# Node tiles worked off inside the first edge loop of a two-layer graph network on one Trainium2 core

## What is computed

```python
# layer 0: edge weights from edge_attr_8, messages from f[src], summed at dst
h = gelu(ea8 @ Wfc1 / sqrt(8)); h = gelu(h @ Wfc2 / 8); w = h @ Wfc3 / 8   # w0, w1: 64, w2, w3: 32 columns
gs, gv = f_s[src], f_v[src]; y0, y1 = ea4[:, 0], ea4[:, 1:4]
mid0 = w0 * gs * y0
mid1 = w3 * einsum('euc,ec->eu', gv, y1) / sqrt(3)        # the dot product
mid2 = (w1 * gs)[:, :, None] * y1[:, None, :]
mid3 = w2[:, :, None] * gv * y0[:, None, None]
ns0, ns1, nv2, nv3 = segment_sum(mid*, dst)
res = self_connection(x) + alpha * (sums @ Wl2);  x = layernorm(x + res)
# layer 1: weights from edge_attr_64, messages from x[dst], summed at src
w = relu(ea64 @ W_fc1) @ W_fc2; xs, xv = (x @ W_nl)[dst]; sh = sqrt(3) * ea3 / |ea3|
out = [w0*xs, w3*dot(xv, sh), (w1*xs) sh, w2 xv, w4*cross(xv, sh)]
x = layernorm(x + gate(segment_sum(out, src) / 32 @ W_out + x @ W_skip))
```

## Time and profile before

| | us |
|---|---|
| median of 3 runs | 2751.35 |
| lowest and highest | 2736.01, 2775.7 |
| the profiled execution | 2767.32 |
| its span, first to last instruction | 2765.5 |
| POOL busy | 2063.6 |
| DVE busy | 1649.6 |
| ACT busy | 899.5 |

### The profile page before, as it was taken

The page is one execution under the profiler, slowest core; times in us unless marked ns, Lnnn a source line. Parts: engine busy times, 40 slices in busy tenths (PEclk is TensorE's granted clock), DMA queues, the critical chain, the costliest instruction groups (busy, mean ns, idle before and its releaser), DMA issues.

```text
span 2765.5 us, 80992 instructions
## 1 busy us (share of the span) xinstructions
PE 2655.6 (96%) x24330; PEld 2250.7 (81%) x24330; DVE 1649.6 (60%) x4264; ACT 899.5 (33%) x2015; POOL 2063.6 (75%) x1856
## 2 busy tenths in 40 slices
PE   4799999999999999999999999999999999999996
PEld 2477777777777777979999999999999999999993
DVE  5365555556555555526666666666666666666664
ACT  1111111111111112224444444444444444444442
POOL 3477777777777775247888888888888888888884
PEclk9999799889989898659999999999999999999998
DMA  4343343333433333247888888888888888888877
GB/s 132 111 110 105 100 109 106 100 104 105 108 103 105 105 105 85 104 173 142 141 144 144 141 144 143 144 143 143 143 142 143 143 144 142 144 144 142 144 124 189
DMA packets 388993, 355.59 MB, mean 129 GB/s; under 512 B 60992, under 2 KB 340928, under 8 KB 388416
## 3 DMA queue, kind: packets, MB, share of 16 engines
q0 software_dynamic: 150528, 141.40, 34.9%
q1 hardware_dynamic: 234816, 209.69, 27.2%
q10 hardware_dynamic: 3616, 4.11, 0.6%
HBM read 244.75 MB, written 135.90 MB: 138 GB/s over the span
## 4 chain that ended last, share of the span: by engine, by line
PE 65%; POOL 16%; issue 11%; DMA 3%; DVE 1%; DVEq 0%; ACT 0%; SPq 0%; POOLq 0%; ACTq 0%
POOL gat L693 15%; PE ps_o L1062 13%; PE ps_w L1050 12%; PE ps_d L1071 10%; PE ps_o L1060 9%; PE ps_x L1084 6%; PE ps_g L909 4%; PE ps_x L1024 3%; DMA gat<-f,gidx 2%; PE ps_w L935 2%; PE ps_h L928 1%; PE ps_h L923 1%; PE ps_r L981 1%; DMA tab<-summed,sidx 1%; PE ps_y L998 1%
## 5 line engine op out<-in xcount | busy, mean ns | idle before, releaser
L740 POOL DMA_INDIRECT tab<-summed,sidx x784 | 1218.6, 1554 | 264.5 <-issue 212.7
L693 POOL DMA_INDIRECT gat<-f,gidx x784 | 751.8, 959 | 244.8 <-issue 232.0
L1291 DVE TENSOR_TENSOR prod<-ps_w,xg 128x768 f32<-128x768 f32 x392 | 375.4, 958 | 244.5 <-PE ps_w L1050 226.7
L1062 PE MATMUL ps_o<-ro_v,prod 128*128 128x96 f32 x3136 | 478.5, 275 | 0.0
L1062 PEld LDWEIGHTS ps_o<-ro_v,prod 128*128 128x128 f32 x3136 | 413.3, 192 | 0.0
L1050 PE MATMUL ps_w<-hid,wf 64*128 64x128 f32 x4704 | 369.3, 290 | 2.0 <-ACT hid L864 2.0
L863 ACT ACTIVATE xg<-ps_x 128x768 f32<-128x768 f32 x392 | 296.3, 808 | 198.8 <-PE ps_x L1084 189.4
L1050 PEld LDWEIGHTS ps_w<-hid,wf 64*128 64x128 f32 x4704 | 294.1, 188 | 70.2 <-issue 44.6
L1071 PE MATMUL ps_d<-msg,same 128*128 128x193 f32 x1568 | 332.5, 334 | 0.7 <-ACT summed L882 0.7
L1060 PE MATMUL ps_o<-ro_s,prod 96*128 96x96 f32 x1568 | 330.2, 292 | 0.6 <-DVE msg L1302 0.6
L909 PEld LDWEIGHTS ps_g<-sel,ta 128*128 128x128 f32 x1568 | 210.0, 209 | 95.0 <-issue 59.2
(11 more groups left out here) (198 smaller groups left out, 3416.9 us busy)
## 6 DMA issues: line engine op xcount, KB each, us to landing
src_bc<-in_src_rows SPq DMA_DIRECT2D x196, 256.0 KB
tabw<-feat SPq DMA_DIRECT2D x784, 36.0 KB
ea<-in_ea SPq DMA_DIRECT2D x196, 128.0 KB
feat<-fst SPq DMA_DIRECT2D x25, 576.0 KB, 2.9
gat<-f,gidx POOLq DMA_INDIRECT x784
hot_dst<-in_dst_rows SPq DMA_DIRECT2D x98, 128.0 KB
hot_dir<-sh_rows SPq DMA_DIRECT2D x98, 128.0 KB
dst_bc<-hot_dst SPq DMA_DIRECT2D x196, 64.0 KB
```

Source lines behind the costliest of these rows:

```text
L693: pool.indirect_dma_start(out=gat[:, r % 4, k, :], out_offset=None, in_=t["f0"], in_offset=bass.IndirectOffsetOnAxis(ap=gidx[:, r // 4, at ...
L740: pool.indirect_dma_start(out=t["tabs"][into[k]], out_offset=bass.IndirectOffsetOnAxis(ap=sidx[:, r, k:k + 1], axis=0), in_=summed[:, r, k ...
L1062: last = pe.matmul(ps_o[:, k, 96 + 64 * c:192 + 64 * c], prod[:, ur % 2, k, 1 + c, :], ro_v[:, c, :], start=True, stop=True)
L1291: dve.tensor_tensor(prod[:, r % 2, :, :, :].rearrange("p k c e -> p k (c e)"), ps_w4[:, :, 0:3 * P], xg[:, r // 2, r % 2 * 2:r % 2 * 2 + 2 ...
```

## The change

- **Node tiles under the edge loop.** `PER` = 8 groups make a period, and in each period one node tile is taken through its steps: DVE copies its sums to `tile_sums` (`node_parts`), PE `update`, DVE `node_update`, `node_scale` and `node_norm` (three Newton steps from an integer first guess in place of ACT's root), PE `turn`, DVE `node_turned`, PE `project`, DVE `node_staged`; ACT then makes the `feat` rows (nine activations) and issues their store. This takes tiles 0 to 22. Tiles 23 and 24 are updated after the loop and finished in the first steps of layer 1. The check in the prologue now also asks that each group's first node lies within `STEP * SLACK` = 48 of an even spread.
- **Join 2 and the node phase go.** SP loads edges, sources, window and hot rows of the first groups before the one join that stays. All weights are loaded at groups 1 to 7, and scaled on ACT at groups 6 and 14; the edge vectors' norms are worked out at groups 4 to 14.
- **Dot product ahead of the sums.** `vy` = gathered vectors times y1, `dot` = its sum over the components, `wy` = w2 times y0; `tb` now holds the three components of the w2 product and the dot product. PE's sums are two sets in place of three, and DVE adds once, to one `acc`.
- **f0 first.** PE makes f0 for all tiles with four banks, and then the self connection with three; xt is loaded in five chunks, weights first; `ROOT_AT` = 6; and POOL issues the gathers of groups 0 to 3 in the prologue.
- **An unread matmul of 256 columns per group** before PE waits for DVE's products.
- Buffers of layer 1 (`prod`, `same`, `sg`, `upd` and those of the early loads) lie in others' places; `ps_h1` and `ps_h2` share a bank, so `layer1` waits for the second gelu of the group before; the scatters begin with tables 2 and 3.

```diff
-ROOT_AT = 10
+ROOT_AT = 6
+PER = 8
+STEP = P // PER
+SLACK = 3
+TIN = (NGRP - 20) // PER + 1
+TSTAGE = (NGRP - 29) // PER + 1
+LAST = NT - 2
...
                 def products(u, j, r):
-                    dve.wait_ge(w_ready, u + 1)
                     dve.wait_ge(gath[r], 16 * G * (j + 1))
...
+                    dve.tensor_tensor(vy[:, :, :, :], gv, y[:, bass.ds(u * G, G), 1:4].unsqueeze(3).to_broadcast([P, G, 3, V]),
+                                      ALU.mult).then_inc(vy_done, 1)
+                    dve.wait_ge(w_ready, u + 1)
                     dve.tensor_tensor(ta[:, h, :, :, :], ps_w[h][:, :, 0:2 * S].rearrange("p k (a s) -> p k a s", a=2),
                                       gat[:, r, :, 0:S].unsqueeze(2).to_broadcast([P, G, 2, S]), ALU.mult)
-                    for dst, at in ((tb, 2 * S), (tc, 2 * S + V)):
-                        last = dve.tensor_tensor(dst[:, h, :, :, :],
...
+                    dve.tensor_tensor(wy[:, :, :], ps_w[h][:, :, 2 * S:2 * S + V],
+                                      y[:, bass.ds(u * G, G), 0:1].to_broadcast([P, G, V]), ALU.mult).then_inc(wy_done, 1)
+                    dve.wait_ge(vy_done, u + 1)
+                    dve.tensor_reduce(dot[:, :, :], vy[:, :, :, :].rearrange("p k c u -> p k u c"), AX.X, ALU.add).then_inc(dot_done, 1)
+                    dve.wait_ge(wy_done, u + 1)
+                    dve.tensor_tensor(tb[:, h, :, 0:3, :], wy[:, :, :].unsqueeze(2).to_broadcast([P, G, 3, V]), gv, ALU.mult)
+                    dve.wait_ge(dot_done, u + 1)
+                    dve.tensor_tensor(tb[:, h, :, 3, :], ps_w[h][:, :, 2 * S + V:2 * S + 2 * V], dot[:, :, :],
+                                      ALU.mult).then_inc(prod_done, 1)
...
 PE, fast:
+                            since(pe, acc_done, u - 1)
+                            idle_matmuls(pe, ps_g[ur % 2][:, 0:2 * P], ident[:, :], 1, 2)
                             pe.wait_ge(sel_ready, u + 1)
                             pe.wait_ge(prod_done, u + 1)
-                            since(pe, acc_done, u - 1)
-                            window_sums(pe, ur, agg_done)
+                            window_sums(pe, ur % 2, agg_done)
...
+                        tile = j - 2
+                        if not isinstance(tile, int) or 0 <= tile < TIN:
+                            if r == 0:
+                                update(tile)
+                            if r == 4:
+                                turn(tile, 0)
+                            if r == 6:
+                                project(tile, 0)
-                    split_steps(pe, NGRP, 3, step)
+                    split_steps(pe, NGRP, 3, step, PER, peel=3 * PER)
...
 DVE, fast:
+                        if r == 5 and (not isinstance(j, int) or 0 <= j - 1 < TIN):
+                            since(dve, acc_done, s - 1)
+                            node_parts(j - 1)
+                        tile = j - 2
+                        if not isinstance(tile, int) or 0 <= tile < TIN:
+                            if r == 0:
+                                node_update(tile, 0)
+                            if r == 1:
+                                node_scale(tile, 1)
+                            if r == 2:
+                                node_norm(tile, 1)
+                            if r == 4:
+                                node_turned(tile, 0)
+                            if r == 6:
+                                node_staged(tile, 0)
...
+                def node_parts(u):
+                    settled(dve, r_ready, u, passed)
+                    here = bass.ds(u * P, P)
+                    dve.tensor_copy(tile_sums[:, :, :], acc[:, :, here]).then_inc(part_done, 1)
...
 ACT, in gelus; tile = j * 2 + r // PER - 3:
+                        if r % PER == 2:
+                            spread_rows(tile, 0)
+                        if r % PER == 3:
+                            spread_plus(tile, 0)
+                        if r % PER == 4:
+                            spread_minus(tile, 0)
+                            send_rows(tile, 0)
```

More of the change, by code:

```diff
@@ L734, in scatter @@
                 def scatter(u, j, r):
-                    into = [(r * 2 + k) % NTAB for k in range(2)]
+                    into = [(r * 2 + k + 2) % NTAB for k in range(2)]
+                    if isinstance(u, int) and u == 1:
+                        pool.wait_ge(skip_out, 16 * 2 * NC)
                     for k in range(2):
@@ L853, in _ @@
+                steps(act, NGRP, gelus, 32, 16)
+                for u in range(TSTAGE, LAST):
+                    stage(u, 0)
                 act.wait_ge(ro_ok, 11)
                 act.drain().then_inc(joined, 1)
-                act.wait_ge(joined, 5 * 2)
+                act.wait_ge(joined, 5)
                 def gathered(g, r):
@@ L1020, in hidden @@
-                def hidden(g, r, turn):
-                    pe.wait_ge(ea_in[r], 16 * (turn + 1))
+                    pe.wait_ge(r_ok, 6)
+                    pe.wait_ge(wn_in2, 16 * 8)
+                    pe.wait_ge(acc_done, NGRP * SWEEP)
+                    for u in range(NT):
+                        since(pe, y_done, u)
+                        update_last(u, 0)
+                        turn(u, 0)
+                        project(u, 0)
+                def hidden(g, r, times):
+                    pe.wait_ge(ea_in[r], 16 * (times + 1))
@@ L1054, in step @@
                             ahead(s, j, r)
+                            if nodes_left:
+                                for u in range(LAST, NT):
+                                    turn(u, u - LAST)
+                        if nodes_left and isinstance(s, int) and s == 2:
+                            project(NT - 1, 1, NT)
+                            pe.wait_ge(y_done, NT)
                         u, _, ur = lagged(s, j, r, 1, 4)
@@ L1272, in second_layer @@
[L1272 to L1278 removed]
+                    done[0] = 0
+                    for _ in range(NT):
+                        dve.sem_inc(row_ready, 1)
@@ L1387, in _ @@
                     fast()
[L1388 to L1390 removed]
+                    join()
                     second_layer(None)
```

910 lines of the change are left out of this document (494 added, 416 removed).

## The result

| | before | after |
|---|---|---|
| median (lowest to highest) | 2753.38 (2736.01 to 2775.7), 4 runs | 3309.2 (3296.16 to 3330.09), 4 runs |
| profiled span | 2765.5 | 3294.7 |
| mean granted clock of the span | 0.938 | 0.758 |

The changed kernel takes 1.202 times as long (95% interval 1.190 to 1.214): 556 us more, where I had forecast 98 less. A later repeat gave 1.204 (1.197 to 1.212).

What follows compares the result with a forecast made beforehand. POOL's gathers were taken to bound the first layer's edge loop, with PE hidden behind them. The terms -131 - 12 + 6 + 30 + 9 gave -98 us, 2653 us on the median, range 2600 to 2725.

Steps and rivals of the forecast that it cites:

- 3, "Is POOL still the bound?": Edge loop: PE at 4.7 us and DVE at 4.4 to 4.9 per group stay hidden under POOL's 4.99; 6 us charged.
- Rival C: Edge loop: PE's waits for DVE inside tile steps cost the clock, half clock at 8.9 us per group, 2837 us; 8%.
- A: Edge loop: no port toll, POOL's pace stays 4.99, prologue and opening at their good ends, -141, 2610 us; 16%.
- B: Edge loop: DVE's chain or the port sets the pace, about 70 us instead of 30, 2700 us; 15%.
- D: Edge loop: the check on each group's first node fails and the general path runs, far slower; 1%.
- Node phase out: Between edge loop and second layer: 141.9 us shrink to 11, gain 131, bounds 125 and 136.
- Prologue: Before the edge loop: f0's own loop and a smaller ROOT_AT gain 12 us, bounds 4 and 20.
- The 6 us for loads and norms on the first groups: Edge loop, groups 1 to 14: weight loads and edge norms while PE is slow, 6 us charged, 0 to 15.
- Port toll: Edge loop: DVE operations with both sources in SBUF hold up POOL's gathers, 30 us more, upper end 73.
- Opening and rest of the second layer: Second layer's start: last two tiles and delayed second scatter cost 9 us, 4 to 20; the rest unchanged.
- the remaining 1470 us: Second layer after its opening: the same instructions, so no change in time.

Runs made afterwards that it cites:

- experiment 6's third version: Changed kernel with its new sums and up to 768 unread columns a step, sized to fill every step to POOL's pace: 2755.84 us, 1.003.
- experiment 4: Kernel before with the dot product ahead of the sums alone, no tile work, no unread matmul: 3190.15 us, 1.166; on a slow chip 3227.37 beside 3215.68.
- experiment 6: Changed kernel with the old sums back under the node tiles, unread matmul left out: 2756.36 us, 1.005; two further versions fill PE's steps with unread matmuls.
- experiment 5's second version: Kernel before with the dot product ahead of the sums, plus four unread matmuls of 72 columns per group: 2907.34 us, 1.059.
- Experiment 3: Changed kernel with all node tiles worked after the edge loop, unread matmul kept: 3565.97 us, 1.299; on a slow chip 3568.61 beside 3215.68.
- experiment 5: Kernel before with the dot product ahead of the sums, plus unread matmuls per group: one of 256 columns 3358.93 us, 1.224; four of 72 columns 2907.34, 1.059.
- experiment 7: Changed kernel, old sums, unread matmul in five of eight steps, more unread matmuls at the start, weight loads spread: 2698.44 us, 0.983; slow chip 3285.01, 1.018.
- experiment 6's first two: Changed kernel with the old sums: without unread matmul 2756.36 us, 1.005; with 256 unread columns in the five steps without tile work 2723.82, 0.995.

## Why the prediction was wrong

**The step that failed is 3, "Is POOL still the bound?"**, in its silent assumption: it priced PE at full clock only. The price itself holds: 4.33 us per group measured, 4.29 predicted, and VectorE, forecast at 4.4 to 4.9 us per group, is busy 319.3 of 400 us in experiment 6's third version, about 4.3. What I took for granted was the sentence above it, that PE "falls behind, works without a gap, regains full clock". The rows of before show this return, but not what it hangs on. The rework of the sums, which I entered as -0.72 + 0.65 us, took the return away: 8.15 us per group instead of 4.33, and 602.9 us more in the edge loop. By experiment 4 this part alone does it in the kernel before (+450), and by experiment 6 the old sums bring it back in the changed one (-538, with the unread matmul out as well). Most of it lies in PE's smaller work and not in VectorE's new chain: experiment 5's second version leaves that chain as it is and regains 283 of the 450 us. What in this work the clock goes by is open.

**Rival C had the end, and not the cause.** Its place (half clock in the edge loop), its price (8.9 us per group, measured 8.22) and its sign (mean clock under 0.8) came true; at nearly all groups at half clock its own formula gives 196 x (8.22 - 5.08) more. A and B don't arise, since POOL isn't the bound, and D didn't happen. I gave C 8%, since I had tied it to the waits in the tile steps and let the unread matmul and PE's own repair speak against it. Experiment 3 takes the tile work away and the loop is at half clock all the same; and in experiment 5 the unread matmul is no help against it. The waits are one way to fall. In the changed kernel one reads:
```profile
1192.62 0.93 PE L991 MATMUL ps_w<-w,h 64*128 64x192 f32 x8
1196.34 0.27 PE L1018 MATMUL ps_p<-ident,x1b 128*64 128x128 f32 x1 [2.79 <-DVE x1b L1346]
...
1198.36 1.86 PE L964 MATMUL ps_g<-sel,ta 128*128 128x96 f32 x8
```
PE waits 2.79 us for the tile's norm, and the next sums take 1.86 instead of 1.03 us. But the kernel before fell too, and came back.

**Step by step.**
1. *Node phase out*, -131: **right behind the join, too large as a whole**. From the join to the first product I forecast 6 us and it is 8.5, so this stretch gains 133.4. But from the last gather to the join it loses 17.9, where I had charged 5: together -115.5, outside my bounds of 125 and 136. And the stretch that I had read was a long one: in the second profile of the kernel before, the same stretch takes 126.6 us (1100.66 to 1227.3) and not 141.9. "From the last matmul to the product some 20 us" is too short, though: from the last gather to the product there are 40.4 us, since PE is still behind at the end and the last tiles stand alone.
2. *Prologue*, -12: **wrong**, group 4's gather comes at 110.6, not at 98. The squares of the directions' second part start after 8.35 us of waiting for their load, where it was 6.50:
```profile
66.82 1.26 SPq L276 DMA_DIRECT2D f<-in_ea_rows  x3
70.60 0.56 DVE L429 TENSOR_TENSOR f<-f 112x384 f32<-112x384 f32 x1 [8.35 <-DMA f<-in_ea_rows]
```
   I had named this second part as what ends the prologue, and that its load waits for the first part's store, and then priced it by `ROOT_AT` and the tiles ahead of it.
3. The bound: above. The 6 us for loads and norms on the first groups can't be told apart in the changed kernel; the slow start and the bunched loads cost 25 us in the version of experiment 7.
4. *Port toll*, +30: **right in size, without weight**. The mean gather rose from 959 to 994 ns with the median at 947, as predicted ("990 or more"): (994 - 959) x 768 = 27 us, and it costs nothing since POOL waits for PE. The new sums bring it: with them but no tile copies the mean is 1001 and 1006 (experiment 4's two runs), with the copies but the old sums 969 and 964 (experiment 6's first two). That fits the added VectorE operations with both sources in SBUF, which weren't tried one by one. So the copies, which I had put at 0.6 us for both and at up to 14 us by the rule of the Trainium skill (SBUF — State Buffer, "SBUF: two separate sides"), cost 768 x 0.005 to 0.010 = 4 to 8, though the larger alone takes 0.82 us.
5. *Opening and rest of the second layer*, +9: **too small**, +41.2. The first scatter comes 24.3 us after the first product instead of 11.2: 13, within the bounds. The other 28 are in "the remaining 1470 us", which "are the same instructions". They nearly are, but off the slow chips the 392 edge factors (`ash`) take 1478 to 1487 us from first to last in every trace with the changed second layer, and 1453 in every trace with the old one, as here in the changed kernel and in experiment 4:
```profile
L1472 DVE TENSOR_TENSOR ash<-ps_o,sh x392: 345/357/359, 1738.9 to 3224.0; 128x192 f32<-128x192 f32 x196
```
```profile
L1293 DVE TENSOR_TENSOR ash<-ps_o,sh x392: 357/358/358, 1672.7 to 3125.6; 128x192 f32<-128x192 f32 x196
```
   A scatter takes 1567 ns in the changed kernel in place of 1554, and ACT waits 315 us for scattered tables instead of 82. The order of the tables and the places of the buffers differ; which of them it is was not tried.

With the clock held and the old sums kept, what is left of the change gives -47 us on the medians (experiment 7), where I had -98. Of the missing 51, 22 are the execution that I read: it lay that much above the median of 2745.13 beside experiment 7. The spans differ by 2696.4 - 2765.5 = -69, 29 short of -98: 29 lost in the second layer (37.8 instead of 9), 12 in the prologue and 10 around the join (-121.3 instead of -131), and 22 gained in the loop (13.8 us more instead of 36).

## What to carry to other kernels

Price TensorE's work at both clocks, and ask of a change not only how long PE works at full clock but whether it gets back there after a fall: a kernel whose PE oscillates between the two levels is near an edge, and less work for PE can leave it at half clock, as here at 450 us of 2740. Look for a stretch at half clock without a gap: there the bound is PE, whatever the full-clock price says. A remedy is unread work that leaves PE no wait in any step, sized step by step, and it has to be measured on more than one chip. In a trace, check the clock's row against the duration of a matmul that is known, above all where the row starts with full clock.

## What was not expected of the hardware

- 400 us and more of PE without a gap at half clock (600 to 1000 us of the changed kernel: busy 400.00, clock 0.50). The Trainium skill (TensorE: Matmul & The Clock Gate, 'Part 1: The HAM clock gate (the "warmup" mystery)') says that activity releases the throttle; in these 400 us it did not, nor in the 1400 us of the loop of experiment 4. The measurement decides.
- Two streams of the same length per group, 8.15 us at half clock: the one with twelve sums comes back to full clock after 3 to 37 us, the one with eight sums and 256 unread columns stays down for up to 850. Four unread matmuls of 72 columns brought 283 us, one of 256 columns cost 169 (experiment 5). What the chip goes by is not settled by these runs.
- The same kernel takes about 2740 us on most chips and 3200 on two. In the traces of these two, PE, ScalarE and VectorE stop for over 3 us at a time in stretches at full clock in the loop, and loops at half clock are as fast as elsewhere (experiment 7). The version of experiment 7 is 1.7% faster than the kernel before on the one kind and 1.8% slower on the other.
- A clock that never rose is shown as 1.00 in the windows (experiment 4).
